# Layer 1's weights prepared in slices inside other stages of a two-layer transformer kernel

## What is computed

```python
x = x + tanh(g_xattn[0]) * L0_xattn(layernorm(x), ctx, causal, padding, ...)   # 32 heads of 8, 8 groups of keys
x = x + tanh(g_ffn[0])   * L0_ffn(layernorm(x), w_up, w_down)      # Hadamard, 8-bit rows, ternary weights, relu^2
x = x + tanh(g_xattn[1]) * L1_xattn(layernorm(x), ctx, ...)        # fp8 rows, 16 heads of 128, self and context
x = x + tanh(g_ffn[1])   * L1_ffn(layernorm(x), Wr, Win, Wout)     # 8 experts, the best 2 of each row
# in L1_xattn:
q  = _ln(fp8_linear(ln_out, wq,  wq_scale,  q_in_scale).reshape(b, s, g, hpg, d))
qx = _ln(fp8_linear(ln_out, wqx, wqx_scale, qx_in_scale)...); k = _ln(fp8_linear(..., wk, ...)); v = fp8_linear(..., wv, ...)
kx, vx = split(einsum('bsi,oi->bso', cond, w_kv_x)); kx = _ln(kx)
cat = concat([gqa(q, k, v), gqa(qx, kx, vx)])
return einsum('bsi,oi->bso', div_clamp_fp8(cat, proj_smooth), wproj) * (proj_in_scale * proj_w_scale)
```

## Time and profile before

| | us |
|---|---|
| median of 3 runs | 1544.68 (1542.19 to 1545.15) |
| the profiled execution, its own time | 1543.84 |
| its span, first to last instruction | 1542.1 |
| TensorE busy | 1286.5 (83%) |
| VectorE busy | 1073.2 (70%) |
| ScalarE busy | 918.4 (60%) |
| GpSimd busy | 690.6 (45%) |
| mean granted TensorE clock, as a share of full speed | 0.922 |

### The profile page before, as it was taken

How to read it: one execution, slowest core, us unless ns; L and a number is a source line. 1 busy time by engine, 2 the same in 40 slices (tenths; PEclk the granted TensorE clock), 3 DMA queues, 4 the chain that set the end, 5 groups by cost and what they waited for, 6 DMA issues and landing times. The chain is left out here.

```text
span 1542.1 us, 29387 instructions
## 1 busy us (share of the span) xinstructions
PE 1286.5 (83%) x8832; PEld 945.2 (61%) x8847; DVE 1073.2 (70%) x2339; ACT 918.4 (60%) x3555; POOL 690.6 (45%) x996
## 2 busy tenths in 40 slices
PE   1699999999940079999999999999999995429991
PEld 0234444444320058888888888888888884429991
DVE  2545665665538858888888888888888877845554
ACT  0144444444522488888888888888888882413330
POOL 2112332332225246665666666656655552643331
PEclk9899999999975579999999999999999997559996
DMA  4322222221005695000000000000000003523325
GB/s 119 58 46 44 43 39 40 42 38 38 8 1 191 222 310 155 1 0 0 0 0 0 0 0 0 0 0 0 1 2 1 2 1 119 159 73 81 93 77 163
DMA packets 118450, 83.49 MB, mean 54 GB/s; under 512 B 66013, under 2 KB 112094, under 8 KB 117600
## 3 DMA queue, kind: packets, MB, share of 16 engines
q1 hardware_dynamic: 114336, 74.04, 18.2%
q0 software_dynamic: 3744, 8.43, 1.5%
q10 hardware_dynamic: 288, 0.00, 0.0%
HBM read 50.01 MB, written 34.00 MB: 54 GB/s over the span
## 5 line engine op out<-in xcount | busy, mean ns | idle before, releaser
L1276 POOL TENSOR_TENSOR head_rstd<-head_rstd,minus_half 128x4 f32<-128x4 f32 x192 | 242.0, 1261 | 15.0
L1266 ACT ACTIVATE squares<-ps 128x128 bf16<-128x128 f32 x768 | 201.4, 281 | 54.1 <-PE ps L1238 43.9
L1238 PE MATMUL ps<-w_proj_in,xq 128*128 128x512 f16 (+1 forms) x1024 | 210.5, 328 | 4.8 <-DVE xq L1225 4.2
L1333 ACT ACTIVATE prob<-ps,nmax 128x128 f32<-128x128 f32 x512 | 182.4, 383 | 11.8 <-DVE nmax L1326 11.8
L1346 POOL TENSOR_TENSOR prob<-prob,rinv 128x512 f32<-128x512 f32 x128 | 135.3, 1057 | 116.2 <-DVE rinv L1341 114.7
L1296 ACT ACTIVATE headsT<-ps,head_ln 128x256 f32<-128x256 f32 (+1 forms) x256 | 166.0, 674 | 27.7 <-PE ps L1289 27.7
L1266 ACT ACTIVATION_READ_ACCUMULATOR squares<-ps 128x1 f32 x768 | 163.1, 213 | 0.0
L1282 DVE TENSOR_TENSOR heads_n<-ps,head_rstd 128x512 f32<-128x512 f32 x192 | 131.5, 685 | 37.5 <-POOL head_rstd L1276 37.5
L562 DVE TENSOR_REDUCE nmax<-ps 128x4 f32<-128x512 f32 x128 | 87.6, 687 | 86.1 <-PE ps L555 85.5
L1319 PE MATMUL ps<-headsT 128*128 128x128 f32 x1024 | 135.2, 275 | 0.0
L1238 PEld LDWEIGHTS ps<-w_proj_in,xq 128*128 (+1 forms) x1024 | 100.6, 98 | 51.2 <-DVE xq L1225 4.6
(11 more groups left out here) (300 smaller groups left out, 2718.8 us busy)
## 6 DMA issues: line engine op xcount, KB each, us to landing
slots<-blank_slot SPq DMA_DIRECT2D x36, 516.0 KB, 10.1
taken<-slots SPq DMA_DIRECT2D x23, 258.0 KB
raw<-in_wprojT SPq DMA_DIRECT2D x4, 1024.0 KB, 6.0
raw<-in_winT SPq DMA_DIRECT2D x4, 1024.0 KB, 8.0
raw<-in_woutT SPq DMA_DIRECT2D x4, 1024.0 KB, 5.7
back<-picked SPq DMA_DIRECT2D x8, 512.0 KB, 7.6
q_stack<-q_parts SPq DMA_DIRECT2D x48, 64.0 KB
k_blocks<-k_parts SPq DMA_DIRECT2D x192, 16.0 KB
```

What stands on the lines that cost most here:

```text
L1238: last = e.matmul(out, xq[:, k, which, slot_at], wb[:, k, hl, w_at + c0:w_at + c0 + n], start=(k == 0 and hl == 0), stop=(k == KD - 1 and ...
L1266: last = e.activation(squares[:, 4 * n + h, :], A[n][:, h * HD1:(h + 1) * HD1], ACT.Square, scale=HD1**-0.5, accum_out=hss[:, 4 * n + h:4 ...
L1276: e.tensor_tensor(hr[:, four], hr[:, four], t["half"][:, four], ALU.pow).then_inc(g_r[n].sem, 1)
L1333: last = e.activation(prob[:, kind, h, :], S[kind][:, h * P:(h + 1) * P], ACT.Exp, bias=nmax[:, kind, h:h + 1], accum_out=rowsum[:, kind, ...
```

## The change

The blocks that prepared layer 1 are gone. In their place:

- **Input weights**: sixteen units of 128 x 1024 (row half k = i % 2, one eighth of the columns of all six matrices), one in each batch of layer 0. LW (SyncE, six transfers), WM (VectorE, sums of six heads), WC (GpSimd: scale the sums, subtract, multiply by the input scales), WH (ScalarE, high half), WL (GpSimd, low half). The loads alternate between two buffers. `wb` becomes [128, 2, 16 units, 1024], is allocated before layer 0, and layer 0's raw ternary weights borrow its last units.
- **ORDER0** is written out again with these pieces. The list starts at another point of the cycle; the transposes F7 come after the up-projection F4u, with the bank waits to match. The padding mask becomes bf16.
- **Constants**: their seven small transfers go into layer 0's first block, the chain (`layer1_constants`) behind VectorE's last batch. A block of its own clears the semaphores.
- **Context halves**: CL, CH, CO once a batch in layer 1's rounds, for two batches at a time.
- **Output weights**: WP, eight pieces of 128 x 1024, in the flat part ahead of layer 1's loop on SyncE, VectorE (high, a copy) and GpSimd (low); O waits for them in the first batch.
- **Fills**: one transfer a batch (BL), 16 in all, for the 36 at the start.
- **A** reads its weights from two units, two runs of half the width.

```diff
@@ ORDER0 (gpsimd, sync; the other engines' lists likewise)
-    "gpsimd": "XB+ F4v-- F7s--- F5v-- F1g- F3b- P1g++++ PD++ MK+++ VC++",
-    "sync": "ROW-- INT- OUT INS CT+++",
+    "gpsimd": "XB WC F5v--- F4v--- F1g-- MK+ F3b-- F7s--- WL VC+ P1g+++ PD+",
+    "sync": "ROW- INT CT++ OUT+ LW+ INS+",
@@ ORDER0, tensor
-        "F4u-- PV:1 OT- S:4+ PV:2 S:5+ W- P2t+++ S:6+ PV:3 S:7+ ST:4 F7d--- F5-- ST:5 OB:0 NT+ P3+++ "
-        "F6-- ST:6 PV:4 F2t- ST:7 PV:5 PV:6 S:0++ F3- S:1++ PV:7 ST:0+ ST:1+ S:2++ OB:1 S:3++ ST:2+ F4- "
-        "F7-- ST:3+ PV:0+"
+        "S:7 F5--- ST:4- ST:5- OB:0- NT F6--- P3++ F2t-- ST:6- PV:4- PV:5- ST:7- PV:6- S:0+ F3-- PV:7- "
+        "ST:0 ST:1 S:1+ OB:1- S:2+ F4-- ST:2 ST:3 F4u-- PV:0 OT- PV:1 S:3+ S:4+ PV:2 S:5+ F7--- W- "
+        "P2t+++ S:6+ PV:3 F7d---"
@@ layer 0, new pieces
+    @s.piece("LW", "sync")
+    def _(e, i, p):
+        e.wait_ge(g_ulow.sem, g_ulow.at(i - 2))
+        e.wait_ge(d_unit.sem, d_unit.at(i - 1))
+        for name, c0, w in UNIT_PARTS:
+            e.dma_start(unit[:, p, c0:c0 + w], a[name][p * P:(p + 1) * P, bass.ds(i * (w // 2) - p * (w // 2), w)]).then_inc(d_unit.sem, 16)
+    @s.piece("WM", "vector")
...
+        e.tensor_reduce(wsum[:, p, :], unit[:, p, 0:CENTRED * HD1].rearrange("p (h d) -> p h d", h=CENTRED),
+                        AX, ALU.add).then_inc(v_usum.sem, 1)
+    @s.piece("WC", "gpsimd")
...
+        e.tensor_tensor(wsum[:, p, :], wsum[:, p, :], share[:, :], ALU.mult).then_inc(g_umean.sem, 1)
...
+        e.tensor_tensor(centred, centred, spread(wsum[:, p, :], HD1), ALU.subtract).then_inc(g_uflat.sem, 1)
...
+        e.tensor_tensor(byhead, byhead, spread(wscale[:, p, :], HD1), ALU.mult).then_inc(g_unit.sem, 1)
+    @s.piece("WH", "scalar")
...
+        e.activation(t["wb"][:, HI, bass.ds(i, 1), :].rearrange("p u c -> p (u c)"), unit[:, p, :], ACT.Copy).then_inc(a_uhigh.sem, 1)
+    @s.piece("WL", "gpsimd")
...
+        e.tensor_tensor(t["wb"][:, LO, bass.ds(i, 1), :].rearrange("p u c -> p (u c)"), unit[:, p, :],
+                        t["wb"][:, HI, bass.ds(i, 1), :].rearrange("p u c -> p (u c)"), ALU.subtract).then_inc(g_ulow.sem, 1)
@@ ORDER1 (the words added)
+    "scalar": "... SC:0 SC:1 CH@0+ TQ:2+ ST:1+",
+    "gpsimd": "RS@2++++ R:1+ SU:1++ CO@3++ SU:2+++ SU:0+++ R:0++",
+    "sync": "CL@0+ BL@1",
@@ A
+        def weights(k, hl, c0, n):
+            return wb[:, hl, 4 * j + k:4 * j + k + 3:2, c0:c0 + n // 2]
@@ output weights, in the flat part before the loop
+    @s.piece("WP", "vector")
...
+        e.tensor_copy(wp[:, 0, four(n), :], wp_raw[:, n % WP_RING, :, :]).then_inc(wp_high, 1)
+    @s.piece("WP", "gpsimd")
...
+        e.tensor_tensor(wp[:, 1, four(n), :], wp_raw[:, n % WP_RING, :, :], wp[:, 0, four(n), :], ALU.subtract).then_inc(wp_low, 1)
+    OUTPUT_AFTER = {
+        "sync": (("CL", 0, -4),) + (("WP", 0),) * 7,
+        "vector": (("RQ", 0, -2, 4), ("WP", 0), ("N", 0, 0, 0, 0), ("N", 0, 0, 0, 1), ("N", 1, 0, 1, 2), ("N", 1, 0, 1, 0),
+                   ("PT", 0, 0, 0, 0), ("N", 1, 0, 1, 1)),
+        "gpsimd": (("SU", 0, 0, 0, 0), ("SU", 0, 0, 0, 1), ("SU", 1, 0, 1, 0), ("R", 0, 0, 0, 1), ("SU", 1, 0, 1, 1), ("SU", 2, 0, 2, 0),
+                   ("R", 1, 0, 1, 1), ("SU", 2, 0, 2, 1)),
+    }
@@ program
+        with nc.Block() as block:
+            @block.gpsimd
+            def _(e):
+                e.sem_clear(spent)
```

More of the change, by code:

```diff
@@ L319, in _ @@
             e.tensor_scalar(pad_key[:, :], padT8[:, :], MASKED, None, ALU.mult)
+            for n, heads in enumerate((slice(0, 2), slice(2, 4), slice(4, 5), slice(6, 7))):
+                width = heads.stop - heads.start
+                e.tensor_copy(wscale[:, :, heads], t["insc"][:, :, n:n + 1].to_broadcast([P, KD, width]))
+            e.memset(wscale[:, :, 5:6].rearrange("p k o -> p (k o)"), CTX_UP)
+            e.memset(wscale[:, :, 7:8].rearrange("p k o -> p (k o)"), CTX_UP)
+            e.memset(share[:, :], 1.0 / HD1)
             e.drain()
@@ L1237, in project @@
                 for hl in range(2):
-                    last = e.matmul(out, xq[:, k, which, slot_at], wb[:, k, hl, w_at + c0:w_at + c0 + n],
+                    last = e.matmul(out, xq[:, k, which, slot_at], weights(k, hl, c0, n),
                                     start=(k == 0 and hl == 0), stop=(k == KD - 1 and hl == 1))
@@ L1244, in project_context @@
                 for part, hl in ((0, 0), (0, 1), (1, 0)):
-                    last = e.matmul(out, cx[:, k, part, rows_at], wb[:, k, hl, w_at + c0:w_at + c0 + n],
+                    last = e.matmul(out, cx[:, k, part, slot_at], weights(k, hl, c0, n),
                                     start=(k == 0 and part == hl == 0), stop=(k == KD - 1 and part == 1))
@@ L1420, in layer1_attention, with _ @@
     filled = t["filled"] = nc.alloc_semaphore("slots_filled")
[L1422 to L1426 removed]
+    @s.piece("BL", "sync")
+    def _(e, b, i):
+        rows = t["slots"].rearrange("(n q p) w -> n p q w", n=FILLS, p=P)[bass.ds(b, 1)].rearrange("n p q w -> (n p) q w")
+        e.dma_start(rows, t["blank"][:, :].unsqueeze(1).to_broadcast([P, SLOTS // (FILLS * P), SLOT])).then_inc(filled, 16)
@@ new lines, in layer1_attention, with four, _ @@
+    wp_got = [nc.alloc_semaphore(f"wp_got{n}") for n in range(WP_RING)]
+    wp_high, wp_low = nc.alloc_semaphore("wp_high"), nc.alloc_semaphore("wp_low")
+    def four(n):
+        first = n // 2 * 4 + n % 2 * 16
+        return slice(first, first + 4)
+    @s.piece("WP", "sync")
+    def _(e, n):
+        if n >= WP_RING:
+            e.wait_ge(wp_low, n - WP_RING + 1)
+        e.dma_start(wp_raw[:, n % WP_RING, :, :], a["wprojT"].rearrange("(h p) o -> p h o", p=P)[:, four(n), :]).then_inc(wp_got[n % WP_RING], 16)
@@ L1431, in layer1_attention, with starting @@
+    def starting(owner):
+        steps = []
+        after = list(OUTPUT_AFTER.get(owner, ()))
+        n = 0
+        for step in part(owner, -AHEAD, 1):
+            steps.append(step)
+            while n < len(after) and (after[n] == step or after[n][0] == "WP"):
+                steps.append(("WP", n))
+                n += 1
+        assert n == len(after), (owner, after[n:])
+        return steps
     with nc.Block() as block:
-        s.run(block, lambda owner: ([("blank",)] if owner == "sync" else []) + part(owner, -AHEAD, 1),
+        s.run(block, starting,
```

265 lines of the change are left out of this document (121 added, 144 removed), and 3 rows, old and new, of the table ORDER1.

## The result

| | before | after |
|---|---|---|
| median, us | 1544.91 (4 runs, 1542.19 to 1545.7) | 1503.5 (4 runs, 1502.52 to 1503.74) |
| the profiled execution, us | 1543.84 | 1503.44 |
| its span, us | 1542.1 | 1501.7 |
| TensorE / VectorE / ScalarE / GpSimd busy, us | 1286.5 / 1073.2 / 918.4 / 690.6 | 1295.5 / 1051.3 / 914.1 / 774.3 |
| mean granted clock, share of full speed | 0.922 | 0.937 |

The account below looks back on a forecast made before the run. TensorE bounds both loops, with nothing to do in the hole between layers. Against 1543.84 us, -67.7 + 4.5 + 6 + 8 + 2 = -47.2 gives 1496.6, say 1497 us, range 1478 to 1524.

Parts of the forecast that it names:

- The bound and the hole: TensorE fills both loops; of the 75.7 us between the layers without TensorE work, 67.7 us would be saved.
- 1 + 0.4 + 2.9: New hole, beside the 3.7 us chain: semaphore clearing 1, one more block boundary 0.4, last block to first statistics 2.9 us.
- Layer 0's start: Seven small transfers (+3.0) and six unit issues (+1.5) on SyncE delay layer 0's first batches: +4.5 us, between 2 and 7.
- Layer 0's loop: Sixteen units' work mostly hidden under TensorE; VectorE delayed 0.4 us a batch by GpSimd: +6 us, from 0 to 40.
- my rate per element: GpSimd's price in layer 0's loop: 2.8 ns an element with two full operands, so 2.9 us for a 1024-wide low half.
- My upper bound: GpSimd's new work in a layer 0 batch: at most 3 x 3.39 + 0.2 = 10.4 us, against 6.8 forecast.
- GpSimd stretches layer 0: Rival: VectorE waits for long GpSimd instructions in layer 0's loop, some 1.5 us more a batch, 1521 us; chance 0.18.
- Layer 1's start: Eight output weight low halves, 23 us on GpSimd against 14 free in about three rounds: +8 us, from 0 to 20.
- my sign of being right: In layer 1's start, the first output projection comes 40 to 47 us after the first projection instead of 35.
- 1512, all in line: Rival: layer 1's start takes all new work in line, 23 us instead of 8; inside the forecast's reach, no separate chance.
- Layer 1's loop and the two-piece reads: Layer 1's rounds: context pieces and fills hidden by TensorE, +2 us, from 0 to 8; weight reads in two pieces cost nothing.
- The rival that would have made the kernel slower: Two-piece weight reads lengthen layer 1's projection matmuls; at 40 ns each, 1569 us; chance 0.04.

Follow-up runs that it names:

- Runs 5 to 7: Edits of layer 0's start in the kernel after: run 5, run 6, then small transfers and first unit loaded from ScalarE's queue in the first block, 1497.61 us.
- run 5: Kernel after, layer 1's small constant transfers issued from ScalarE, the unit's loads in layer 0's loop put behind the keys' reading back: 1508.06 us.
- run 6: Kernel after with both moves of run 5, and VectorE summing the raw ternary weights ahead of its first unit sum: 1500.32 us.
- Run 9: Kernel after with extra 128x1024 GpSimd subtractions on idle tiles in each batch of layer 0: two, 1504.89 us; four, 1586.2 us.
- run 1: Kernel after with SyncE issuing the second context load ahead of the last four output weight loads: 1494.87 us, ratio to before 0.9675.
- run 3: Kernel after with the edit of run 1, and the output weights' low halves subtracted on VectorE instead of GpSimd: 1487.76 us, ratio to before 0.9626.

## Why the prediction was right, and which terms were off

**The bound and the hole: right.** The hole was the only stretch without TensorE work that the change touches, and 68.4 us of it went, 67.7 forecast. The new hole is 7.3 us, 8.0 forecast: the chain 3.7 as copied from the earlier trace rows, the first statistics 1.7 us behind the next block's first issue. The clearing and both boundaries lie in the 1.9 + 1.7 = 3.6 us from the chain's end to the first statistics, where I had 1 + 0.4 + 2.9.

**Layer 0's start: right in kind and size** (+5.6 for +4.5). Runs 5 to 7 show that it was three waits behind one another, of which I had named the two on SyncE. I did not look at which VectorE instructions are queued behind the unit's sum in the first batch: the ternary weights' sum (run 5) and the second batch's row maxima (run 6).

**Layer 0's loop: less than forecast.** The 15 steps between the first and last up-projection take 331.9 us instead of 330.9, +1.0 where I had +6 for 16 batches; 1.6 more went in the first batches. GpSimd's work is 5.7 us a batch instead of 6.8, mostly because the low half takes 2126 ns and not 2.9 us: my rate per element came from instructions of 256 columns, with their fixed part. Here the Trainium skill had it: page "GPSIMD Engine Reference", section "Performance versus the Vector engine", gives 4497 ns for an addition over 2048 columns of f32, by my estimate from it 2.2 ns a column, and this case shows 2126 / 1024 = 2.08. My upper bound, 3.39 us for such an instruction, was GpSimd held up by VectorE (see the last section).

**The mechanism of the rival "GpSimd stretches layer 0" is there, but hidden.** (It is the second in my list; one sentence calls it the first.) VectorE's instructions do stretch beside GpSimd: the normalisation of the rows (source view, before and after)

```profile
L429 DVE SCALAR_TENSOR_TENSOR xn<-x_rows,mv_p,rstd_p x16: 467/468/483, 33.3 to 350.3; 128x256 f32<-128x256 f32 x16
```

```profile
L449 DVE SCALAR_TENSOR_TENSOR xn<-x_rows,mv_p,rstd_p x16: 468/1127/1205, 36.8 to 360.5; 128x256 f32<-128x256 f32 x16
```

takes 1127 ns instead of 468, and nothing waits for it. Run 9 sets the distance: two more long GpSimd instructions a batch still cost nothing to speak of, four make the kernel slower than before. The forecast of a small cost was right, with less than 8.5 us to spare.

**Layer 1's start: the step that failed.** I costed it as GpSimd work that does not fit, +8, from 0 to 20; it was +18.7, and my sign of being right, a first output projection 40 to 47 us after the first projection, failed with 54.0. Of the 18.7, 8.5 us is a wait that I did not price at all (run 1): I wrote of the context only "a load", and did not ask what stands ahead of the second one on SyncE. That the 10.2 left lie close to my +8 is in part luck: only 5.6 of them are shown to come from the low halves on GpSimd (run 3), 4.6 are open, and with the 2.13 us that a low half takes my own sum gives 8 x 2.13 - 14 = 3. The ring of four and the order of one line in the diff were enough to see it. The rival "1512, all in line" gave 23 for this term by the wrong mechanism. The sum came out only 6.8 us too low (1496.6 against the profiled 1503.44), since 4.8 of this term's 10.7 were given back by 3.4 us too much in layer 0's loop and 1.4 in layer 1's; that too is luck.

**Layer 1's loop and the two-piece reads: right.** +0.6 us over 63 rounds. The projections' matmuls take 329 ns on the mean, against 328 before:

```profile
L1241 PE MATMUL ps<-l_wb,xq 128*128 128x512 f16 (+1 forms) x1024 | 211.0, 329 | 13.7 <-ACT headsT L1299 9.1
```

Their fastest and median, 272 and 379 ns, are those of before to the nanosecond. The rival that would have made the kernel slower did not come about.

## What to carry to other kernels

When work moves into a running pipeline, price three things apart: its busy time, what is queued behind each new wait on every engine that gets one, and what stands ahead of each small transfer on the queue that issues it. One load behind a ring of buffers cost 8.5 us here, more than the 5.6 us that the eight subtractions on GpSimd are shown to have cost. And an engine's wait for the answer to something that it made itself is no free time for work that stands elsewhere in its list: subtract such waits before you compare its work with the length of a batch, and shift a little more work onto it on purpose to see at what amount the time breaks.

## What the runs showed of the hardware

- VectorE's copy of 1024 columns takes 0.68 us alone and 2.0 beside a GpSimd subtraction. Rows of the kernel after, layer 1's start:

```profile
494.20 2.13 POOL L1454 TENSOR_TENSOR w_proj_out<-w_out_raw,w_proj_out 128x1024 f16<-128x1024 f32 x1
```

```profile
494.88 2.01 DVE L1449 CAST w_proj_out<-w_out_raw 128x1024 f16<-128x1024 f32 x1
...
503.53 0.68 DVE L1449 CAST w_proj_out<-w_out_raw 128x1024 f16<-128x1024 f32 x1
```

  The copy that begins at 494.88 ends at 496.89, 0.56 us behind the end of GpSimd's instruction, where it takes 0.68 alone: it was held for nearly all of it. GpSimd's eight took 2.12 to 2.13 us each, unstretched. This agrees with the Trainium skill, page "SBUF — State Buffer", section "SBUF: two separate sides": a GpSimd instruction and a VectorE instruction with two SBUF inputs or in a two-port mode lock the shared port pair against each other, whole instruction by whole instruction, and the first to start has it. In which mode this copy ran no run here shows. I had not expected that an f32 to f16 copy, with one input, would be held too.
- Contrary to what I had written behind the earlier trace rows, not every VectorE instruction on SBUF is held, and GpSimd can be the one that loses. Rows of the kernel before, where GpSimd subtracts without a gap from 474.41 to 485.77:

```profile
477.97 1.21 DVE L1101 TENSOR_REDUCE head_sum<-raw 128x8 f32<-128x1024 f32 x1
479.21 2.56 DVE L1102 TENSOR_SCALAR head_sum<-head_sum 128x8 f32<-128x8 f32 x1
...
489.16 1.28 DVE L948 SCALAR_TENSOR_TENSOR w_proj_in<-raw,in_scales,w_proj_in 128x1024 f16<-128x1024 f32 x1
```

```profile
489.33 2.86 POOL L1066 TENSOR_TENSOR raw<-raw,head_sum 128x1024 f32<-128x1024 f32 x1 [3.56 <-DVE head_sum L1102]
```

  The reduction takes 1.21 us beside GpSimd (all four of its shape 1.21 on the mean), the scaling behind it 2.56 instead of 0.17. And GpSimd's subtraction that begins 0.17 us behind one of VectorE's takes 2.86 us and ends 1.75 us behind it; with a broadcast operand of the same width it took 1.90 in the kernel after.
- The same subtraction over 1024 columns takes 1225 ns on VectorE and 2126 ns on GpSimd.
- When TensorE began to wait in the loop (four extra subtractions) the granted clock fell from 1.00 to 0.91 on the mean of 130 to 440 us, and the mask's matmuls took 459 ns on the mean (300 to 412 us), against 384 in the kernel after (300 to 400). How much of the 76 us this made, no run separates.
